# Moving one image's output projection, routing and row sends to other steps of the next image's loop, and two weight loads ahead of the fills

## What is computed

```
x = x + gate(groupnorm(x)) * groupnorm(x)
t = tokens(x)                                  # 16 x 1024 x 128
q, k, v, d = split(layernorm(t) @ W_qkv)
t = t + concat(softmax(q k^T / 4) v, decay @ d) @ W_out + b_out
n = layernorm(t);  logits = n @ wg + bg        # 8 experts, the best two, softmax of the two
t = t + sum over the two: gate_e * (relu(n @ w1[e] + b1[e]) @ w2[e] + b2[e])
```

## Time and profile before

| what | us |
|---|---|
| median of 3 runs (2399.57 to 2407.99) | 2407.72 |
| the profiled execution, whole | 2410.66 |
| its span, first to last instruction | 2408.8 |
| TensorE busy in the span | 2077.7 |
| VectorE busy | 1906.1 |
| ScalarE busy | 1458.6 |
| GpSimd busy | 1019.7 |
| mean granted TensorE clock | 0.938 |

### The profile page before, as it was taken

The page is one execution under the profiler, slowest core; times in us unless marked ns, Lnnn a source line. Parts: engine busy times, 40 slices in busy tenths (PEclk is TensorE's granted clock), DMA queues, the critical chain, the costliest instruction groups (busy, mean ns, idle before and its releaser), DMA issues.

```text
span 2408.8 us, 35243 instructions
## 1 busy us (share of the span) xinstructions
PE 2077.7 (86%) x11552; PEld 959.4 (40%) x11552; DVE 1906.1 (79%) x3669; ACT 1458.6 (61%) x2897; POOL 1019.7 (42%) x1479
## 2 busy tenths in 40 slices
PE   2699999999999999999999999999999267778743
PEld 1233333334343343334343333333333146666633
DVE  5767799999999999899999999999971356666732
ACT  1126787777778778677777768777775024444420
POOL 2101224352525344251535435154133646777764
PEclk9999999999999999999999999999996579999975
DMA  5320321322322122232312123222012178666759
GB/s 171 55 46 1 54 45 37 90 47 51 66 45 63 35 56 45 52 63 46 66 28 62 39 52 59 53 60 44 12 55 79 36 227 280 199 210 205 209 186 341
DMA packets 100991, 215.06 MB, mean 89 GB/s; under 512 B 30225, under 2 KB 50393, under 8 KB 100377
## 3 DMA queue, kind: packets, MB, share of 16 engines
q1 hardware_dynamic: 78000, 166.96, 28.3%
q0 software_dynamic: 17280, 35.95, 4.2%
q10 hardware_dynamic: 5528, 9.91, 1.2%
HBM read 104.30 MB, written 61.23 MB: 69 GB/s over the span
## 4 chain that ended last, share of the span: by engine, by line
PE 58%; DVE 15%; POOL 9%; DMA 7%; issue 6%; ACT 3%; ACTq 1%; SPq 1%; POOLq 0%; DVEq 0%
PE ps L879 21%; PE ps L891 18%; DVE row_max L1418 10%; POOL y_dram L765 6%; PE ps L858 4%; PE ps L835 3%; DMA y_dram<-region 2%; DMA big<-w_dram 2%; ACT region L1168 2%; DMA region<-y_dram 2%; PE ps L843 2%; PE ps L847 1%; PE ps L923 1%; PE ps L899 1%; PE ps L830 1%
## 5 line engine op out<-in xcount | busy, mean ns | idle before, releaser
L1418 DVE TENSOR_REDUCE row_max<-ps 128x1 f32<-128x512 f32 x2048 | 1293.6, 682 | 141.2 <-PE ps L858 127.7
L1168 ACT ACTIVATE region<-ps 128x512 f32<-128x512 f32 x2048 | 1095.0, 601 | 409.3 <-PE ps L879 403.1
L858 PE MATMUL ps<-big 48*128 48x512 f32 x2048 | 836.4, 479 | 48.8 <-DVE row_max L1418 31.4
L879 PE MATMUL ps<-big 50*128 50x512 f32 x2048 | 776.2, 463 | 32.8 <-ACT region L1168 22.5
L879 PEld LDWEIGHTS ps<-big 50*128 50x128 f32 x2048 | 327.0, 192 | 663.0 <-ACT region L1168 493.4
L891 PE MATMUL ps<-region 128*32 128x512 f32 x4096 | 574.6, 634 | 0.0
L858 PEld LDWEIGHTS ps<-big 48*128 48x128 f32 x2048 | 347.6, 194 | 151.5 <-DVE row_max L1418 121.6
L765 POOL DMA_INDIRECT y_dram<-region x284 | 271.9, 957 | 119.6 <-issue 83.0
L710 POOL DMA_INDIRECT xs_dram<-region,slot x256 | 249.7, 975 | 81.2 <-issue 71.9
L1019 PE MATMUL ps<-big 128*128 128x512 f32 x284 | 125.5, 442 | 76.8 <-DMA big<-w_dram 76.2
L646 POOL TENSOR_TENSOR norm_v<-norm 128x8 f32<-128x8 f32 x32 | 6.7, 210 | 410.1 <-DVE norm L1407 410.0
(11 more groups left out here) (183 smaller groups left out, 2033.8 us busy)
## 6 DMA issues: line engine op xcount, KB each, us to landing
big<-w_dram SPq DMA_DIRECT2D x71, 514.0 KB, 4.6
big<-q_parts SPq DMA_DIRECT2D x384, 64.0 KB, 2.4
big<-k_parts SPq DMA_DIRECT2D x372, 64.0 KB, 2.4
region<-xs_dram SPq DMA_DIRECT2D x71, 264.0 KB, 2.8
region<-y_dram SPq DMA_DIRECT2D x16, 1024.0 KB, 10.0
region<-in_x SPq DMA_DIRECT2D x28, 512.0 KB, 5.2
t_dram<-region SPq DMA_DIRECT2D x16, 512.0 KB, 3.4
out<-region ACTq DMA_DIRECT2D x16, 512.0 KB, 6.0
```

The source lines that it names most:

```text
L858: pe.matmul(ps[:, M_BANK + half % M_BANKS, :], lane_rows(q_stack[k % 2], h, SHIFT_ROW)[:, t * P:(t + 1) * P], lane_rows(k_stack[k % 2], h, ...
L879: pe.matmul(ps[:, E_BANK + score % E_BANKS, :], lane_rows(k_stack[k % 2], h, STACK)[:, t * P:(t + 1) * P], lane_rows(q_stack[k % 2], h, ST ...
L1168: act.activation(probs[:, u % 2, step_head(k, s, i), :], ps[:, E_BANK + score % E_BANKS, :], ACT.Exp, scale=DH ** -0.5).then_inc(exp_done, 1)
L1418: dve.tensor_reduce(row_max[:, c, h * TILES + t:h * TILES + t + 1], ps[:, M_BANK + half % M_BANKS, :], AX.X, ALU.max).then_inc(max_done, 1)
```

## The change

- `project_out` goes from steps 33 and 37 to 11 and 13, `turn_t2` from 41 and 43 to 19 and 21, the logits from 51 to 29, the choosing from 52 to 58 (every step) to 31 to 43 (every other step), `exp_gap` from 60 to 45, `gates` from 62 to 47, `dispatch` from 63 to 49.
- The projections of image `it + 2` go later: q from 19 and 21 to 23 and 25, k from 23 and 25 to 33 and 35 (from loop 1 on; loop -1 keeps the old steps). One `vz` goes from 49 to 51, and one k of loop 0 from 51 to 49.
- GpSimd does `normalise2` and `mark` of image `it - 1` ahead of `split` and `add_decayed`, and sends the rows of image `it - 1` at the end of loop `it`. Its loop ends one `it` earlier.
- SyncE asks for the weights of blocks 0 and 1 as soon as the table is there, ahead of the fills; waits that these loads need stand ahead of them.

```diff
-AT_PREP = ((1, 3), (15, 17), (19, 21), (23, 25))
-AT_PREP_LATE = ((25, 27), (37, 39), (41, 43), (51, 55))
+AT_PREP_FIRST = ((1, 3), (15, 17), (19, 21), (23, 25))
+AT_PREP = ((1, 3), (15, 17), (23, 25), (33, 35))
+AT_PREP_LATE = ((25, 27), (37, 39), (41, 43), (49, 55))
...
-AT_OUT = (33, 37)
+AT_OUT = (11, 13)
...
-AT_TURN_T2 = (41, 43)
-AT_LOGITS = 51
+AT_TURN_T2 = (19, 21)
+AT_LOGITS = 29
 AT_TURN_O = (31, 47, 53)
-AT_VZ = (45, 49, 59, 61)
+AT_VZ = (45, 51, 59, 61)
...
-AT_DISPATCH = 63
+AT_DISPATCH = 49
...
-AT_GAP = 60
-AT_PICK = (52, 53, 54, 55, 56, 57, 58)
-AT_GATES = 62
+AT_GAP = 45
+AT_PICK = (31, 33, 35, 37, 39, 41, 43)
+AT_GATES = 47
...
             sp.wait_ge(table_done, 1)
+            sp.wait_ge(score_ready, 2 * IMAGES * STEPS)
+            sp.wait_ge(w_saved, 32)
+            for b in range(XS_AHEAD):
+                load_weights(b)
             for e in range(EXPERTS):
...
-                if 0 <= b - XS_AHEAD:
+                if XS_AHEAD <= b - XS_AHEAD:
                     load_weights(b - XS_AHEAD)
...
-            for it in range(-1, IMAGES + 2):
+            for it in range(-1, IMAGES + 1):
...
-                if 0 <= it - 2:
-                    slots(it - 2)
+                if 0 <= it - 1:
+                    normalise2(it - 1)
                 if it + 2 < IMAGES:
                     split(it + 2, 0)
-                if 0 <= it - 2:
-                    send_second(it - 2)
-                if it + 2 < IMAGES:
                     split(it + 2, 1)
+                if 0 <= it - 1:
+                    mark(it - 1)
                 if 0 <= it < IMAGES:
                     add_decayed(it)
...
-                if 0 <= it - 1 < IMAGES:
-                    normalise2(it - 1)
-                    mark(it - 1)
+                if 0 <= it - 1:
+                    slots(it - 1)
+                    send_second(it - 1)
```

## The result

The changed kernel takes 2372.31 us (median of 4 runs, 2359.02 to 2376.83) where the kernel before takes 2407.24 beside it: a ratio of 0.984, 95% interval 0.980 to 0.988. It is 1.5% faster. The forecast was 2403, no change that can be told, and a range of 2380 to 2430: the time lies under its lower end. Run once more behind the experiments it has 2370.85 beside 2408.23.

What follows compares the result with a forecast made beforehand. No engine was taken to bound a usual loop throughout; GpSimd's sends bound from the first block on. 2410.66 - 14.3 - 0.2 + 0 + 1 + 9 = 2406.2, as a median 2403 us, range 2380 to 2430.

Steps and rivals of the forecast that it cites:

- The tail, -14.3: Behind the last loop: ScalarE's copy of image 15's turned tokens no longer waits for image 14's rows, -14.3 us.
- First weights, -0.2: At the first block: TensorE's 2.37 us wait goes, but requests ahead of the fills cost some 2.2, so -0.2 us.
- the x load, +1: SyncE's load behind the k stacks: lands 0.1 us late for ScalarE's `affine` at step 48, +1 us over 12 loops.
- The usual loops, 0: Loops 1 to 14: VectorE's work moved between groups of eight steps, sum 93.0 against 92.95 us, so no change.
- Steps 16 to 23: Group in a usual loop: VectorE's 11.71 us plus half the moments, 1.1, gives 12.8.
- Steps 24 to 31: Group in a usual loop: the logits enter TensorE with 2.1 us and VectorE waits, so 13.28 becomes 15.3 us.
- Steps 8 to 15: Group in a usual loop: VectorE is full and gains 1.5 us of `add_attention`, so 12.58 becomes 14.1 us.
- Steps 40 to 47: Group in a usual loop: VectorE loses 2.2 us and gains 1.2, so 12.08 falls to some 11.6 us.
- The clock drops: Usual loops: the 1.5 us a drop cost at steps 48 to 55 is kept, and expected at steps 29 to 32.
- The last loop, +9: Loop 15: +6.5 us from more time at the lower clock, +2.6 from outputs and moments on a full VectorE; +9.
- Faster, 2383: Rival for the usual loops: the clock stays at the higher level, 1.5 us a loop goes 13 times; chance 0.33.
- Slower: Rival, 2421 us: GpSimd's work beside VectorE's scans makes four more collisions, 1.4 us a loop, +18; chance 0.25.

Runs made afterwards that it cites:

- The loads put into this group and into 32 to 39: Changed kernel with six scores computed twice in loops 1 to 14, at steps 18 to 20 (2394.94 us) or at 34 to 36 (2380.38 us).
- the old weights: Changed kernel with the first weights asked for behind the fills again, as before: 2371.21 us, ratio 0.985.

## Why the prediction was wrong

**The tail, -14.3: right.** The copy waits for TensorE; it starts 16.5 us earlier behind the last exponential in the two profiles. The forecast took the turn of t2 to end 15.7 behind the loop's end; in the eight profiles with the new places in the last loop it ends 10.7 to 16.3 behind it, with the clock of those microseconds. Tails are 541.9 and 541.7 with the old places in the last loop, and 522.7 to 533.6, a mean of 527, in these eight. The room for the sends was smaller than the 36 to 47 us worked out: the first starts at 1829.58, 28 us ahead of the copy, 6 us behind step 49, as GpSimd waits for `places` until 1826.91, and the steps from there to the loop's end ran at the higher clock. They take 23.7 from first to last, and the last landed some 2.3 behind its start before (1894.62 to 1896.93), so it was enough, by an estimated 3.

**First weights, -0.2, and the x load, +1: right, within 1 us.** The first is told above. The x load cost nothing: ScalarE waits for no load ahead of `affine` in the two profiles of the changed kernel. It is closer than it was: in loop 9 SyncE asks for it at 1177.38, the landing takes 4.3, and `affine` starts some 2.5 us behind that. It starts without a wait:

```profile
1183.51 1.09 ACT L1170 ACTIVATE region<-ps 128x512 f32<-128x512 f32 x2 [0.57 <-PE ps L881]
1184.48 1.24 ACT L1112 ACTIVATE region<-region,offset,slope 128x1024 f32<-128x1024 f32 x1
```

**The usual loops, 0: the step that failed.** "I move VectorE's pieces between the groups of eight steps." Four things went wrong in it, with the drops a fifth.

- *Steps 16 to 23.* The earlier trace rows have TensorE at 12.56 of 12.56 there and VectorE at 11.71; the forecast added moments to VectorE's number, and took nothing out of TensorE's. Three projections stood here (steps 19, 21 and 23) and one does now; two lighter turns came in: 11.84 against the forecast's 12.8. The loads put into this group and into 32 to 39 show that TensorE binds here.
- *Steps 24 to 31.* The logits' 2.1 us of TensorE were added to the group's length. 14.06 against 15.3; with one eighth of the logits steps 24 to 39 take as long as with all, so most of the 2.1 costs no time here.
- *Steps 8 to 15.* 13.44 against 14.1. Durations were added up as if VectorE ran one instruction after the other. Its maxima last 0.68 and start 0.59 apart; a pair of moments stands for 0.45 and not for 2 x 0.28. VectorE's busy time in the group rose by 0.81, not by 1.5. TensorE is at 13.44 of 13.44 there too, and no run tells which of the two ends it. VectorE in 40 to 47 before, then after (the first line starts just ahead of step 40):

```profile
1625.47 0.47 DVE L1407 BATCH_NORM_STATS2 norm<-region 128x6 f32<-128x128 f32 x2
1625.92 1.29 DVE L1418 TENSOR_REDUCE row_max<-ps 128x1 f32<-128x512 f32 x2
```

```profile
753.18 0.68 DVE L1420 TENSOR_REDUCE row_max<-ps 128x1 f32<-128x512 f32 x1
753.77 0.47 DVE L1471 TENSOR_TENSOR_SCAN region<-fade,region 128x128 f32<-128x128 f32 x1
754.17 1.26 DVE L1420 TENSOR_REDUCE row_max<-ps 128x1 f32<-128x512 f32 x2
755.35 0.22 DVE L1508 TENSOR_TENSOR gate<-gate,gate_v 128x64 f32<-128x64 f32 x1
755.60 0.23 DVE L1509 TENSOR_TENSOR gate<-gate,rank 128x64 f32<-128x64 f32 x1
755.86 1.29 DVE L1420 TENSOR_REDUCE row_max<-ps 128x1 f32<-128x512 f32 x2
757.06 0.47 DVE L1471 TENSOR_TENSOR_SCAN region<-fade,region 128x128 f32<-128x128 f32 x1
```

  The Trainium skill, "VectorE: DVE Perf Modes", section "The DRAIN you can't avoid", says that the next instruction doesn't start until the pipe is empty, and adds that one which nothing holds starts earlier. The trace agrees with the second: a maximum lasts 0.68 and the next instruction starts 0.59 behind it. Behind each instruction of the choosing the program waits for its end, and what follows starts later than it lasts (0.25 and 0.26 for 0.22 and 0.23).
- *Steps 40 to 47.* 13.35 against 11.6, the one miss to the other side. VectorE is behind: the choosing of step 39 runs here, at 755.35, when ScalarE's exponentials have reached step 41, and three scans fall into this group where two did. So the pairs of moments that left were replaced by choosing that costs more for its waits. This is read from the timelines; the run with the choosing spread out bears it out in part, as 32 to 47 fell there from 27.29 to 26.41.
- *The clock drops.* The forecast kept the 1.5 us of one drop and took it for each loop. The price was near: 1.9 before, 1.3 after. What changed is how often: in ten of loops 2 to 12 before, in five of them after. That is 1.14 of the 2.37 us a loop. They come where the forecast put them, behind the logits: from step 30 or 31 on in loops 2 to 14 after, mostly from 52 or 53 on before. How often wasn't to be read from one loop of the profile of before, and none of the rivals had half of the drops.

The misses in the single groups, up to 1.75 us and of both signs, add up to -1.1 a loop; that they cancel so far is luck. With steps 0 to 7 (-0.2) and the drops (-1.1) that is the -2.4 of loops 2 to 12.

Loops 13 and 14 gained nothing (+0.1 and +3.7). No projections stand in loop 14, so the places only move work into full groups: without a drop it takes 101.5 with the new places (in the profile with the old weights) against 100.8, and the rest is a drop of 10.2 us in this profile.

**The last loop, +9: mis-sized.** It was worked out from one execution's clock (0.70). In eight profiles with the new places and nothing else changed in this loop it is 103.8 to 114.9, a mean of 107.6, against 107.7 and 105.4 with the old: about +1, which can't be told from nothing in that spread. The clock of one profile isn't the kernel's.

**The rivals.** *Faster, 2383*, had the right sign and part of the mechanism (fewer drops, and 56 to 63 falling below 13.2, to 12.71). *Slower* by collisions with GpSimd fell: scans of loops 1 to 13, first before, then after (count, busy time in all, mean in ns; the first line of each is the forward ones, the other two the backward ones):

```profile
L1456 DVE TENSOR_TENSOR_SCAN region<-fade,region 128x128 f32<-128x128 f32 x104 | 57.4, 552 | 0.0
L1469 DVE TENSOR_TENSOR_SCAN region<-fade,region 128x128 f32<-128x128 f32 x91 | 48.1, 528 | 0.0
L1469 DVE TENSOR_TENSOR_SCAN region<-fade,tail,region 128x128 f32<-128x128 f32 x13 | 6.3, 484 | 0.5
```

```profile
L1458 DVE TENSOR_TENSOR_SCAN region<-fade,region 128x128 f32<-128x128 f32 x104 | 49.6, 477 | 0.0
L1471 DVE TENSOR_TENSOR_SCAN region<-fade,region 128x128 f32<-128x128 f32 x91 | 52.3, 575 | 0.0
L1471 DVE TENSOR_TENSOR_SCAN region<-fade,tail,region 128x128 f32<-128x128 f32 x13 | 7.9, 610 | 0.5
```

The backward scans take 5.8 us more in 13 loops, the forward ones 7.8 less. In loop 5 the forward scan at step 23 fell from 0.67 to 0.47, since GpSimd's split no longer runs beside it; that at step 13, beside `norm1` before and after, fell from 0.80 to 0.57, and why isn't shown. The forecast had +18 for the collisions that come and nothing for those that go.

**The sum, put right.** -23 for the loops, -15 for the tail, +1 for the last loop, nothing for the rest: 2408 - 37 = 2371, the time measured. Of the 32 us between 2403 and 2371, 23 are the usual loops, 8 the last loop and 1 the x load.

## What to carry to other kernels

When work moves between steps that different engines bind, take out and put in every engine's pieces for each group, from the column that is full there, not those of one engine; cost an instruction by the distance to the next start, not by its duration. An idle load of known size put into one group and then into another tells in two runs which of the two groups that engine binds. What only one profile's clock shows (how often a drop comes, how long a last loop is) needs a second profile, or all loops of the first, before it carries a term.

## What was not expected of the hardware

- How often the clock falls in a usual loop isn't set by the logits alone, though most drops start right behind them. Loops that take 104.7 us without a drop (before; with the load in 16 to 23, worked out as 103.4 + 1.4) have one in 10 to 14 of 14, loops of 103.4 to 103.7 in 5 to 9; but the kernel before with one tile's logits has loops of 103.9 and ten drops. Neither fewer small products nor idle ones among them did away with the drops. The cause stays open, and with it half of the gain in the loops: that the drops became fewer is measured, why is not.
- A busy TensorE isn't one at the higher level: steps 32 to 39 of the last loop have it busy for 22.68 of 23.64 us at 0.50. The Trainium skill, "TensorE: Matmul & The Clock Gate", "Part 1: The HAM clock gate (the "warmup" mystery)", has it that activity releases the lower level; the busy column of these windows doesn't show the activity that it means.
- Idle products of 256 columns and 128 rows, one a step, went with a granted clock of 1.00 from step 40 of the last loop to its end in two profiles of two, with the hidden bias moved away; the same with 512 columns did not in the one profile that there is. The run times of the two overlap, so that the size of the product makes the difference isn't shown.
